# Four-layer kernel: the last batch of the fourth attention goes by halves of queries, with its last half finished on VectorE

## The reference, cut to what matters

```python
# fourth attention: 8 heads, two maps per head, no mask
L1, L2 = cosine logits of (q1, k1), (q2, k2), scaled
G  = tanh(delta_gain * (L1 - L2))
y  = (softmax(L1 + G) - lambda_full * softmax(L2 - G)) @ v
y  = y * rsqrt(mean(y*y over a head's 16 features) + 1e-5) * subln_weight * 0.5
x  = x + y @ Wo.T + bo
# fourth feed-forward, on xt = layernorm(x)
gates = softmax(xt @ wg);  e = argmax(gates)
pos   = how many earlier tokens chose e          # an order over all 4096 tokens
keep  = pos < 512
slot  = e * 512 + pos                            # the token's row is sent there
out   = (relu(xt_slot @ w1[e] + b1) @ w2[e] + b2) * gate * keep
x     = x + out
```

## Time and profile before

| | us |
|---|---|
| median of 3 runs | 3560.78 (3556.45 to 3560.81) |
| the profiled execution, its own time | 3568.88 |
| its span, from the first to the last instruction | 3567.1 |
| the fourth attention's loop, from the first to the last step | 2611 to 3404 |
| from there to the first row load of the experts | 3404 to 3470 |
| the experts of the fourth layer, and the output | 3470 to 3567 |

### The profile page before, as it was taken

The page is one execution under the profiler, slowest core; times in us unless marked ns, Lnnn a source line. Parts: engine busy times, 40 slices in busy tenths (PEclk is TensorE's granted clock), DMA queues, the critical chain, the costliest instruction groups (busy, mean ns, idle before and its releaser), DMA issues. The chain is left out here.

```text
span 3567.1 us, 51582 instructions
## 1 busy us (share of the span) xinstructions
PE 2992.9 (84%) x18320; PEld 1209.2 (34%) x18320; DVE 2607.5 (73%) x6022; ACT 2145.6 (60%) x2739; POOL 486.4 (14%) x753
## 2 busy tenths in 40 slices
PE   5999997896999999985999898947569988889836
PEld 2333333443122222214455555535412222222214
DVE  6999973666999999946666666631868888888821
ACT  2566673223377777773555455512479989999812
POOL 2000001333000000004000000013221011102023
PEclk7899998997799999997999999968779999999958
DMA  5442202333211111000000000012362223221112
GB/s 146 62 108 57 33 13 49 66 78 113 28 27 27 23 22 22 12 5 31 1 1 1 7 1 7 1 62 65 104 124 31 31 33 39 31 29 20 53 28 70
DMA packets 172978, 148.30 MB, mean 42 GB/s; under 512 B 79672, under 2 KB 130632, under 8 KB 172720
## 3 DMA queue, kind: packets, MB, share of 16 engines
q1 hardware_dynamic: 168624, 137.21, 19.5%
q0 software_dynamic: 4096, 7.78, 0.7%
HBM read 95.13 MB, written 49.68 MB: 41 GB/s over the span
## 5 line engine op out<-in xcount | busy, mean ns | idle before, releaser
L1324 ACT ACTIVATE a_probs<-a_scores 128x1024 f32<-128x1024 f32 (+3 forms) x896 | 791.4, 932 | 372.2 <-PE a_scores L1206 235.1
L1347 DVE TENSOR_REDUCE a_part_max<-a_slot_ps 128x1 f32<-128x512 f32 x1280 | 798.5, 683 | 32.7 <-PE a_slot_ps L1184 31.2
L2219 DVE TENSOR_TENSOR a_probs<-a_logit_ps,a_gate 128x1024 f32<-128x1024 f32 x512 | 602.3, 1219 | 102.6 <-ACT a_gate L2078 99.3
L1184 PE MATMUL a_slot_ps<-a_k_op,a_q_op 48*128 48x512 bf16 (+3 forms) x1792 | 579.8, 380 | 90.0 <-PEq L123 28.1
L2083 ACT ACTIVATE a_probs<-a_probs 128x2048 f32<-128x2048 f32 x256 | 488.0, 1906 | 8.5 <-DVE a_probs L2219 4.3
L1206 PE MATMUL a_scores<-a_q_op,a_k_op 51*128 51x512 bf16 (+3 forms) x1792 | 453.3, 362 | 7.1 <-ACT a_probs L1324 6.1
L1226 PE MATMUL a_o_ps<-a_probs,a_v_op 128*32 128x512 f32 (+3 forms) x3584 | 438.6, 561 | 1.2 <-ACT a_o_sb L1311 0.6
L1184 PEld LDWEIGHTS a_slot_ps<-a_k_op,a_q_op 48*128 48x128 bf16 x1792 | 150.2, 94 | 692.5 <-DVE a_part_max L1347 469.4
L1984 PE MATMUL a_logit_ps<-space 96*128 96x512 bf16 x1024 | 303.8, 387 | 73.6 <-DVE a_probs L2219 62.8
L2078 ACT ACTIVATE a_gate<-a_diff_ps 128x1024 f32<-128x1024 f32 x256 | 261.3, 1021 | 59.3 <-PE a_diff_ps L1984 51.3
L1997 PE MATMUL a_o_ps<-a_probs,a_v_op 128*32 128x512 f32 x2048 | 275.7, 610 | 7.0 <-DVE a_o_sb L2212 3.1
(11 more groups left out here) (401 smaller groups left out, 3928.0 us busy)
## 6 DMA issues: line engine op xcount, KB each, us to landing
e_coef<-coef_dram SPq DMA_DIRECT2D x16, 1024.0 KB, 10.1
a_q_op<-scratch_q SPq DMA_DIRECT2D x384, 32.0 KB
a_k_op<-scratch_k SPq DMA_DIRECT2D x384, 32.0 KB
scratch_q<-p_parts SPq DMA_DIRECT2D x24, 384.0 KB, 3.3
scratch_k<-p_parts SPq DMA_DIRECT2D x24, 384.0 KB, 3.5
space<-scratch_k SPq DMA_DIRECT2D x192, 32.0 KB
space<-scratch_g SPq DMA_DIRECT2D x192, 32.0 KB
space<-scratch_q SPq DMA_DIRECT2D x192, 32.0 KB
```

What stands on the lines that cost most here:

```text
L1184: nc.tensor.matmul(out[:, 0:width], q_op[g][r0:r0 + MAX_ROW, e, qt * P:(qt + 1) * P], k_op[g][r0:r0 + MAX_ROW, e, kh * CH:kh * CH + width] ...
L1324: nc.scalar.activation(probs[gs % NB][:, 2 * e:2 * e + 2, off:CH], scores[e][:, :, off:CH], ACT.Exp, scale=scale).then_inc(probs_done, 1)
L1347: nc.vector.tensor_reduce(part_max[u % 2][:, kh, col:col + 1], slot[:, 0:w], axis=AX.X, op=ALU.max).then_inc(slot_done, 1)
L2219: nc.vector.tensor_tensor(probs[gs % 4][:, m, :, :], logit_ps[m][:], gate[gs % 2][:], op) \
```

## The change

The 64 steps of the last batch get another order: all four groups for the first half of the queries (32 steps), then all four for the second half. The work list is now five parts, `PARTS`: batches 0 to 2 whole (8 tiles, the steps of `LONG`, as before), the first half of batch 3 (4 tiles, `HALF`) and its second half (4 tiles, `TAIL`). The second half uses a PSUM bank of its own (`diff_ps`), its squares, both roots, its scaling and its norm run on VectorE, and only its sending on GpSimd. The roots take three rounds in place of four everywhere; VectorE's round has three operations, GpSimd's four. The load of the weights waits for step 240 in place of 224. `Chooser`'s methods work on `n` tiles; for four tiles the prefix sum takes two doublings in place of three.

```diff
@@ CosineShape
-    END = TOTAL + NS
+    END = TOTAL + 18
+    LONG = {"squared": 7, ("t", 0): 13, ("t", 1): 15, ("y", 0): 17, ("y", 1): 20, "sums": (18, 21), "stats": (19, 22), "moments": 23,
+            ("x", 0): 30, ("x", 1): 32, ("l",): 34, "choose": 35, "exp": 36, "mark": 37, "share": 38, ("n",): 39, "assign": (40, 41, 42, 43)}
+    HALF = {"squared": 16, ("t", 0): 20, ("y", 0): 22, "sums": (23,), "stats": (24,), "moments": 24,
+            ("x", 0): 29, ("l",): 31, "choose": 32, "exp": 33, "mark": 33, "share": 34, ("n",): 36, "assign": (38, 38, 41, 41)}
+    TAIL = {"squared": 5, ("t", 0): 5, ("y", 0): 7, "sums": (8,), "stats": (8,), "moments": 8,
+            ("x", 0): 8, ("l",): 10, "choose": 11, "exp": 12, "mark": 12, "share": 13, ("n",): 13, "assign": (14, 15, 16, 17)}
...
+        self.PARTS = [(b * KB, KB, (b + 1) * self.NS) for b in range(BATCH - 1)]
+        self.PARTS += [(TILES - KB, CPT, self.TOTAL - self.NS // 2), (TILES - CPT, CPT, self.TOTAL)]
...
     def where(self, gs):
         b, s = divmod(gs, self.NS)
-        return b, s // self.S, s % self.S // KB, s % KB
+        if b < BATCH - 1:
+            return b, s // self.S, s % self.S // KB, s % KB
+        return b, s % (self.NS // 2) // KB, s // (self.NS // 2), s % KB
@@ cosine_attention
+        def bank(task):
+            if shape.is_late(task):
+                return diff_ps[:, 0, :], late_ready, late_done, shape.place[1][task]
+            return spare_ps[:], spare_ready, spare_done, shape.place[0][task]
...
-            sp.wait_ge(pv_done, TOTAL - NS + 2 * S)
+            sp.wait_ge(pv_done, TOTAL - 2 * KB)
             weights.load(sp)
...
@@ gpsimd
-                for i in range(4):
+                for i in range(3):
...
-            for b in range(BATCH):
+            for i in range(LAST):
+                tile0, n, end = shape.PARTS[i]
...
+                pool.wait_ge(nat_done, end // KB)
...
+                if i > 0:
+                    pool.wait_ge(sent[i - 1], 16 * KB)
...
+                send(i)
+            send(LAST)
@@ vector
+            def inverse_root(v, y, y0, trial, factor):
+                then(nc.vector.tensor_scalar(y0.bitcast(I32), v.bitcast(I32), -0.5, float(0x5f3759df), ALU.mult, ALU.add))
+                for i in range(3):
+                    last = factor if i == 2 else 1.0
+                    then(nc.vector.tensor_tensor(trial, y0, y0, ALU.mult))
+                    then(nc.vector.scalar_tensor_tensor(out=trial, in0=trial, scalar=-0.5 * last, in1=v, op0=ALU.mult, op1=ALU.mult))
+                    then(nc.vector.scalar_tensor_tensor(out=y if i == 2 else y0, in0=trial, scalar=1.5 * last, in1=y0,
+                                                        op0=ALU.add, op1=ALU.mult))
+            def scale_last():
...
+                dve.wait_ge(nat_done, end // KB)
+                then(nc.vector.tensor_tensor(mine, rows, rows, ALU.mult))
+                then(nc.vector.tensor_reduce(mean[:, g], mine.rearrange("p (n g) -> p n g", g=RMS), axis=AX.X, op=ALU.add))
+                then(nc.vector.tensor_scalar(mean[:, g], mean[:, g], 1.0 / RMS, 1e-5, ALU.mult, ALU.add))
+                inverse_root(mean[:, g], inv[:, g], guess[:, g], trial[:, g], 0.5)
+                groups = rows.rearrange("p (n g) -> p n g", g=RMS)
+                nc.vector.tensor_tensor(groups, groups, inv[:, g].unsqueeze(2).to_broadcast([P, n * D // RMS, RMS]), ALU.mult) \
+                    .then_inc(late_scaled, 1)
+            def norm_last():
...
+                dve.wait_ge(moments, LAST + 1)
+                inverse_root(var[:, mine], rstd[:, mine], var_guess[:, mine], var_trial[:, mine], 1.0)
+                dve.wait_ge(sent[BATCH - 2], 16 * KB)
+                for t in range(n):
+                    tile = first + t
+                    ins = nc.vector.tensor_scalar(xr[:, tile, 0:D], x[:, (tile0 + t) * D:(tile0 + t + 1) * D], mv[:, tile, 0:1],
+                                                  rstd[:, tile:tile + 1], ALU.subtract, ALU.mult)
+                ins.then_inc(late_rows_done, 1)
```

More of the change, by code:

```diff
@@ L1782, in choose @@
         dve.wait_ge(bank_done, k + 1)
[L1783 to L1788, removed]
+        then(nc.vector.tensor_reduce(best, logits, axis=AX.X, op=ALU.max))
+        nc.vector.tensor_tensor(shifted, logits, wide(best, EXPERTS), ALU.subtract).then_inc(shares_ready, 1)
@@ L1801, in assign @@
[L1801 to L1805, removed]
+        first_of_max(nc, then, hot, self.logits[:, 0:n, :], best, self.descending, EXPERTS)
+        nc.vector.tensor_copy(self.hot_bf[:, 0:n, :], hot).then_inc(self.hot_done, 1)
@@ L2233, in _ @@
-                if r == 37:
-                    chooser.mark(dve, then, b, shares_ready)
-                if r == 38:
-                    chooser.share(dve, then, b, shares_done)
-                if r in (40, 41, 42, 43):
-                    if r == 40 and b > 0:
-                        dve.wait_ge(sent[b - 1], 16 * KB)
-                    chooser.assign(dve, then, b, r - 40, spare_ps, spare_ready, spare_done, shape.place["n", b], xr, slot_done)
+                for i, _ in shape.due(gs, "squared"):
+                    if i == LAST:
+                        scale_last()
+                    else:
+                        means(i)
@@ new lines, in _ @@
+                for i, c in shape.due(gs, "sums"):
+                    add_rows(i, c)
+                for i, c in shape.due(gs, "stats"):
+                    row_stats(i, c)
+                for i, _ in shape.due(gs, "moments"):
+                    row_moments(i)
+                    if i == LAST:
+                        norm_last()
+                for i, _ in shape.due(gs, "choose"):
+                    ps, ready, done, k = bank(("l", i))
+                    chooser.choose(dve, then, i, ps, ready, done, k, shares_ready, shape.PARTS[i][1])
@@ new lines, in _ @@
+                for i, _ in shape.due(gs, "mark"):
+                    chooser.mark(dve, then, i, shares_ready, shape.PARTS[i][1])
+                for i, _ in shape.due(gs, "share"):
+                    chooser.share(dve, then, i, shares_done, shape.PARTS[i][1])
+                for i, part in shape.due(gs, "assign"):
+                    tile0, n, _ = shape.PARTS[i]
+                    if part == 0 and 0 < i < LAST:
+                        dve.wait_ge(sent[i - 1], 16 * KB)
+                    ps, ready, done, k = bank(("n", i))
+                    chooser.assign(dve, then, part, ps, ready, done, k, xr, slot_done, tile0, n, first_of(i))
```

344 lines of the change are left out of this document (190 added, 154 removed).

## The result

| | before | after |
|---|---|---|
| median of 5 runs, us | 3560.78 (3556.45 to 3571.25) | 3536.16 (3528.59 to 3537.41) |
| ratio, 95% interval | | 0.9919 [0.9907, 0.9930] |
| the profiled execution, its own time | 3568.88 | 3537.41 |
| its span | 3567.1 | 3535.6 |
| first tanh of the loop to its last | 781.0 | 782.1 |

What follows compares the result with a forecast made beforehand. Engines working in turn between the last attention step and the experts' first row load were taken as the bound. Chain gain 29.6 less loop loss 3.2 is 26.4 us: 3560.78 to 3534.4, range 3528 to 3540, up to 3544 with rivals.

Steps and rivals of the forecast that it cites:

- The chain, 30.2 us: After the loop, last square to last sending: four tiles and VectorE take 30.2 us instead of 59.8, gaining 29.6.
- The bounds of 28.5 and 30.5: Range in us for the chain's gain, from other prices for the roots' small VectorE instructions and the router's gain.
- Part 2: First half's router and sendings behind the last step: hidden beside the second half's work, 1.6 us to spare, costing nothing.
- the sign: Sign of being wrong: GpSimd's issues of sendings more than 1.3 us apart beside VectorE's router.
- Part 3: First half's work inside the last batch's loop: a loss of 3.2 us, between 2 and 6.
- the step that held 0.5: At step 240 VectorE's means wait for GpSimd's square of the first half: 0.3 us, taken as 0.5.
- Part 4: New order of the last batch's steps, later weights' load, three root rounds on GpSimd in earlier batches: no price.
- The 1.5 us that I could not assign: Loop stretch with the weights' load took 28.4 us, batch 1's 26.9; whether the load causes this was left open.
- Rival 1: First half's sendings on GpSimd slow beside VectorE's router and delay the last ones: 3538 us, chance 0.08.
- Rival 2: The last batch's loop pays as for a whole batch: 12 us lost, 17.5 saved, 3543 us, chance 0.05.
- Rival 3: TensorE's clock falls in the last batch; slower from 17 low steps, 3582 us with all 32; chance 0.02.
- Rival 4: Second half's chain waits for something of the first; only halved sendings, norms and turns count: 3551 us, chance 0.03.

Runs made afterwards that it cites:

- halves_on_gpsimd: Changed kernel with the second half's square, roots, scaling and norm on GpSimd, the first half sent only behind that norm: median 3539.74 us, ratio 0.9943.
- order_only: Kernel before with only the last batch's new step order, its matching TensorE wait, and the weights' load at step 240: median 3560.65 us, ratio 1.0007.
- whole_on_vector: Changed kernel with the halves undone: last batch whole, old order, weights' load at step 224, small operations still on VectorE: median 3545.17 us, ratio 0.9962.
- copies: Changed kernel with 14 float32 128x512 on-chip copies on VectorE ahead of the second half's choose, beside the first half's sendings: one run, 3537.94 us.
- warm: Changed kernel with unused identity turns on TensorE: 102 in and just ahead of the chain, 88 before the experts: median 3534.28 us, ratio 0.9935.
- warm2: As warm against the changed kernel, but the 88 turns became 80 behind TensorE's last chain job and 10 before the experts: 3531.38 us, ratio 0.9925.
- shift: Changed kernel with the whole batches' router logits two steps later and the first half's jobs one step later: median 3528.61 us, ratio 0.9921.
- warm_shift: Changed kernel with the edits of warm and shift together: median 3527.4 us, ratio 0.9920.

## Why the prediction was right

It said 3534.4 with 26.4 us gained. The first set of runs gave 3536.16 and the average of three ratios 26 us. By the stages, 59.74 - 29.83 - 3.4 = 26.5. The chain's part was right term by term. In the loop's part two errors nearly cancelled, and that it came so close is luck.

- **The chain, 30.2 us.** Measured 29.83, and no term is off by more than about 0.1 us. The 0.3 for three handoffs was unneeded, as the terms, taken from start to start, already held them; so the chain gained 29.9 us where 29.6 was forecast. The bounds of 28.5 and 30.5 don't follow from the prices named for them: with 0.22 for the roots and no gain in the router the gain would be 27.9, with 0.17 for the roots 29.8. The measured 29.9 is inside the stated bounds and just above the second of these. VectorE's scaling ended 4.63 us after the last `nat`, predicted 4.7. The 32-column operations of the root took 0.19, those on 4 columns 0.16, just under the 0.17 taken. The Trainium skill's table (VectorE: DVE Perf Modes, section on the TRN2 errata) would give the first an estimated (58 + 32) / 0.96 = 94 ns; its fit gives 191, and the fit is what the rows show again.
- **Part 2, nothing.** `choose` and `mark` lay in the wait for the last value products, which shrank from 3.19 to 1.31 us; the copy behind it started no later after the last tanh (6.60 us in place of 6.59). The first half's sendings ended 2.0 us before the last of the second half's slot numbers was written, where 1.6 had been worked out. The prediction named issues more than 1.3 us apart beside the router as a sign of being wrong. They were 1.40, 1.27 and 1.28 apart, but the first gap is 1.40 with nothing beside it too (3456.62 to 3458.02 before), so the sign was set too tight.
- **Part 3, 3.2 us.** Measured 3.4, and halves_on_gpsimd, with the same jobs in the loop, has the same 3.4, while order_only and whole_on_vector have none of it. But the step that held 0.5 of the 3.2 was wrong. I had taken the first record of the tanh line for the first step; it is a table load, and every step number was one too high. The earlier trace rows are step 239, not 240, so GpSimd had a step more. In the changed kernel it squared from 3348.49 to 3349.56 and VectorE's reduction came at 3353.18, without a wait:

```profile
3348.49 1.07 POOL L2193 TENSOR_TENSOR a_square<-a_nat 128x512 f32<-128x512 f32 x1
...
3353.18 0.67 DVE L2246 TENSOR_REDUCE a_mean<-a_square 128x32 f32<-128x512 f32 x1
```

  So the wait cost nothing in place of 0.5, and the jobs themselves 3.4 us in place of 2.75. Part of this comes from the same slip, because the stretches that priced the jobs began some 3 us early. On batch 1's true steps the stretch with one `x` turn is 24.4 us and not 24.1 (columns as in the earlier trace rows):

```profile
2875.60:2900.00 24.40, 8.18 (x8) 1.00 0.03 4
```

  With 24.7 and 25.0 for the two others, the jobs would have been priced at 0.8 + 0.95 + 1.3 = 3.05. The other 0.3 us stay open. Of the 3.4, 1.3 lie in the stretch with the turn and the product, and 2.1 in the one with statistics, moments and `x` turn.
- **Part 4, nothing.** Confirmed by order_only. The 1.5 us that I could not assign don't belong to the weights' load: the stretch stays at 28.6 to 28.7 without it. The batches before show such stretches too, of 27.5 to 29.0 us, with no weights beside them, and moving the logits behind the `o` turn took them to 25.0.
- **The rivals.** Rival 1 had more slack than I gave it, and no issue beside the router or beside the long copies was slow enough for it. Rival 2's 12 us of loop were 3.4. Rival 3 needed 17 low steps; the last two stretches show a clock of 1.00. Rival 4 fell with the 2.80 us in which GpSimd waited for the second half alone.

## What to carry to other kernels

When a stage in which several engines take turns sets the end, price it by the start-to-start times of its handoffs and ask of each piece whether it needs all of the data: here halving the part that has to come last brought 17.6 us for 3.4 in the loop, and putting the small dependent operations on the engine that is quickest with them brought 6.5. Count steps from a record that you have seen to be the first of its kind, since one step decides whether a wait exists. Before filling an engine's wait with work, find out what releases the engine: work put behind a meeting point of all engines lengthens what follows it.

## What the runs showed that I had not expected

- **The end of a sending can hold a small VectorE operation.** The copy of 8 columns at 3428.12 took 0.32 us inside GpSimd's sending of 3427.47 to 3428.44; the same operation took 0.17 at 3420.45 with no sending beside it. The one behind it took 0.24 in place of 0.18. Both ended at 3428.44, with the sending, and others earlier in the same sending kept their 0.17. Both other profiles of the changed kernel show the same 0.32, and copies, where no sending lies beside it, 0.17. It cost this chain 0.06 us: 0.36 from the copy to the operation after the next, in place of 0.30.
- **TensorE and SyncE start on the experts together**, at 3428.07 and 3428.15 in warm and 3430.84 and 3430.92 in warm2, some 3.05 us after the last sending's end. That both wait for the same meeting point of the engines, and that it and not the rows' landing ends last, fits these rows; it was not tried by itself and stays open.
- **A short wait of one engine can cost the loop more than its length.** In shift VectorE's wait of 1.25 us stood in a stretch that was 3.5 us longer, with the clock at 0.94 where the changed kernel has 1.00. In warm_shift the same stretch was 3.6 us longer at a clock of 1.00, so the fall of the clock doesn't explain it.
